# Two graph layers over 16 batches on one core: the first layer straight, squarings in six of eight pairs, and the second layer's prologue in the last two

## What is computed

```python
h = jnp.maximum(_layernorm(x), 0.0)
x = x + layer0(h, adj, alpha, w, d, fc_in_w, fc_in_b)
h = jnp.maximum(_layernorm(x), 0.0)
x = x + layer1(h, L=adj, adjacency=adj, ...)

# layer0: eight Euler steps, linear in h
ax = einsum('nm,bmd->bnd', adj, h)
f = alph * 0.5 * (ax - h) + h @ w_eff - h + x0
h = h + dt * f

# layer1
lam_max = eigvalsh(L)[-1] + 1e-08
L_norm = 2.0 * L / lam_max - eye(N)
h = relu(layernorm((L_norm @ x) @ Wc + bc)); x1 = h + x
scores = q @ k.T / sqrt(32)   # four heads, q, k, v = x1 @ Wq, Wk, Wv
attn = softmax(where(adjacency > 0, scores, -1e9))
x2 = layernorm(x1 + (attn @ v) @ Wo + bo)
return layernorm(x2 + gelu(x2 @ W1 + b1) @ W2 + b2)
```

## Time and profile before

| | us |
|---|---|
| median of 3 runs | 965.14 (964.48 to 966.01) |
| the profiled execution | 965.88 |
| its span | 964.1 |
| busy in it: PE, PEld, DVE, ACT, POOL | 885.7 (92%), 724.3 (75%), 653.7 (68%), 552.5 (57%), 325.2 (34%) |
| first layer with its setup | 0 to 443.6 |
| first mask of attention | 454.98 |
| POOL at the opening of the second block: L1682, L1665, L1667 | from 449.73: 1.28, 0.61, and 1.27 from 451.64 |
| landing of one load of x (256 KB), median | 2.8 |

### The profile page before, as it was taken

One profiled execution on the slowest core, in us unless ns is written; L12 is line 12 of the kernel. 1 busy time (PEld: TensorE's weight loads), 2 busy tenths in 40 slices (PEclk: granted clock), 3 DMA queues, 4 the chain that ended last, 5 costly groups with the idle time before them and its releaser, 6 DMA issues.

```text
span 964.1 us, 19623 instructions
## 1 busy us (share of the span) xinstructions
PE 885.7 (92%) x6854; PEld 724.3 (75%) x6854; DVE 653.7 (68%) x2077; ACT 552.5 (57%) x1210; POOL 325.2 (34%) x426
## 2 busy tenths in 40 slices
PE   5999999999999998984999999999999999888993
PEld 4878989898989888864777676767777777666782
DVE  5955343445444445544788888898888888887786
ACT  3223333333333333213888888888888887876574
POOL 3111111111120202121334545554555444313876
PEclk9999999999999998997999999999999999999998
DMA  3000000000000000005555544444445554500122
GB/s 96 0 12 12 12 12 13 11 12 12 11 11 11 22 0 12 1 1 131 131 133 133 133 122 113 110 112 104 110 125 131 132 133 133 130 4 1 47 64 66
DMA packets 47223, 61.61 MB, mean 64 GB/s; under 512 B 4377, under 2 KB 22050, under 8 KB 47138
## 3 DMA queue, kind: packets, MB, share of 16 engines
q1 hardware_dynamic: 46034, 60.38, 24.6%
q10 hardware_dynamic: 1104, 0.13, 0.1%
HBM read 39.53 MB, written 20.97 MB: 63 GB/s over the span
## 4 chain that ended last, share of the span: by engine, by line
PE 56%; DVE 13%; issue 10%; POOL 9%; ACT 7%; DMA 3%; SPq 0%; DVEq 0%; ACTq 0%; POOLq 0%
PE bank L828 10%; PE bank L798 9%; PE bank L790 9%; PE bank L782 6%; PE bank L1738 4%; DVE prob L1908 4%; PE bank L1758 3%; PE bank L694 2%; PE bank L1802 2%; POOL z_gain L333 2%; POOL z_norm L337 2%; DMA q_stack<-bounce_k 2%; ACT prob L1849 2%; PE bank L1725 2%; POOL x_bo L1682 2%
## 5 line engine op out<-in xcount | busy, mean ns | idle before, releaser
L1849 ACT ACTIVATE prob<-prob,low 128x512 f32<-128x512 f32 x256 | 183.9, 719 | 54.1 <-DVE low L1908 52.4
L1908 DVE CUSTOM_DVE_ANT_0 prob<-bank,mask 128x512 f32<-128x512 f32 x256 | 171.1, 682 | 27.0 <-PE bank L1725 25.7
L1738 PE MATMUL bank<-ident,prob 128*128 128x128 f32 x1024 | 161.8, 281 | 12.8 <-ACT probT L1838 12.8
L1738 PEld LDWEIGHTS bank<-ident,prob 128*128 128x128 f32 x1024 | 114.4, 141 | 58.5 <-issue 30.7
L1725 PE MATMUL bank<-k_stack,q_stack 128*128 128x512 f32 x256 | 123.7, 485 | 12.2 <-DMA q_stack<-bounce_k 9.2
L828 PE MATMUL bank<-B_hi,halves 128*128 128x384 f32 x384 | 107.7, 343 | 6.4 <-DVE halves L1176 6.4
L1838 ACT ACTIVATE probT<-bank 128x512 f32<-128x512 f32 x176 | 102.5, 583 | 2.8 <-PE bank L1738 1.1
L620 POOL TENSOR_SCALAR var_eps<-mv 128x4 f32<-128x4 f32 x16 | 3.6, 227 | 295.3 <-DVE mv L1127 295.3
L798 PE MATMUL bank<-halves,P3T_hi 128*128 128x256 f32 x512 | 95.8, 288 | 3.0 <-DVE halves L1194 1.8
L979 ACT ACTIVATE Sq<-bank,trace_inv 128x512 fp32r<-128x512 f32 x64 | 44.0, 687 | 91.4 <-PE bank L782 91.4
L1758 PE MATMUL bank<-probT,v 128*32 128x128 f32 x2048 | 82.3, 279 | 5.0 <-DVE probT L1895 1.7
(11 more groups left out here) (251 smaller groups left out, 1964.9 us busy)
## 6 DMA issues: line engine op xcount, KB each, us to landing
k_stack<-bounce_q SPq DMA_DIRECT2D x64, 256.0 KB, 5.0
q_stack<-bounce_k SPq DMA_DIRECT2D x64, 256.0 KB, 7.5
bounce_q<-k_parts SPq DMA_DIRECT2D x16, 512.0 KB, 2.8
bounce_k<-q_parts SPq DMA_DIRECT2D x16, 512.0 KB, 3.2
x_in<-in_x_dram SPq DMA_DIRECT2D x16, 256.0 KB, 2.8
out_dram<-probT SPq DMA_DIRECT2D x16, 256.0 KB, 2.3
y<-in_adj_dram SPq DMA_DIRECT2D x4, 256.0 KB, 4.3
W1s<-in_L_gnn_W_dram SPq DMA_DIRECT2D x1, 128.0 KB, 2.6
```

The lines of the kernel that those rows point to most:

```text
L1738: last = pe.transpose(psum[2 + u % 2][:, mt * P:(mt + 1) * P], prob[u % RING][:, mt * P:(mt + 1) * P], ident[:, :])
L1849: act.activation(prob[u % RING][:, :], prob[u % RING][:, :], ACT.Exp, bias=low[:, u % TURNED:u % TURNED + 1], scale=-1.0, accum_out=row_su ...
L1908: dve.tensor_tensor_reduce(prob[u % RING][:, :], psum[u % 2][:, :], mask[:, u // HEADS, :], 1.0, 3e38, ALU.add, ALU.min, low[:, u % TURNED ...
```

## The change

The first layer is written straight on all engines: the loops over pairs (and SP's over loads of x) become Python loops. The 16 squarings lie in pairs 0 to 5 (2, 3, 3, 3, 3, 2). What was early work of pair 7 is now in pair 6 (`LAM_PAIR`), and x1's transposes, keys and queries of batch 0 are in pair 7 (`KEY_PAIR`), one after another in bank 7, with waits for `k_lo_ready` and `q_lo_ready` ahead of the next user; values stay in pair 8. POOL takes batch 0's and 1's norm (`z_root`, `norm_z`) within pair 6, between the scales of batches 14 and 15, and h of batch 2 is made in pair 7. In `feature_products` the wait for T_lo[m] moves into the loop over m. The split of L moves from ahead of round 1 to its unit 1 (ACT) and unit 2 (DVE).

```diff
-def pairs(eng, body):
-    for p in range(3):
-        body(p)
-    with eng.Fori(3, LAST_SQUARED + 1) as p:
-        body(p)
-    for p in range(LAST_SQUARED + 1, PAIRS + 1):
-        body(p)
...
+SQUARES = (ROWS_FIRST, ROWS_3, ROWS_3, ROWS_3, ROWS_3, ROWS_2)
+TRACES = (("T0a", "C3a"), *[("T0a", "Y0_0", "C3a")] * 4, ("T0a", "C0a"))
+LAM_PAIR, KEY_PAIR = LAST_SQUARED + 1, LAST_SQUARED + 2
...
                 def pair(p):
-                    if isinstance(p, int) and p == PAIRS - 1:
+                    if p == LAM_PAIR:
                         for b in range(2):
                             h_scales(pool, one, b, b)
...
+                    x_and_bias(2 * p + 1, 1)
+                    if p == LAM_PAIR:
+                        z_root(pool, one, 0)
+                        norm_z(pool, one, 0)
+                        scales(2 * p + 2, 0)
+                        z_root(pool, one, 1)
+                        norm_z(pool, one, 1)
+                    if p < PAIRS - 1:
+                        scales(2 * p + 3, 1)
...
                 def feature_products(b, nt):
-                    if nt == 0:
-                        for m in range(GROUP):
-                            pe.wait_ge(T_lo_ready[m], b + 1)
                     at_least(pe, C_ready, NT * b + nt - 1)
                     for m in range(GROUP):
+                        if nt == 0:
+                            pe.wait_ge(T_lo_ready[m], b + 1)
...
-                    step = (p - (PAIRS - 1), place)
+                    step = (p - LAM_PAIR, place)
...
-                    if step == (0, "C3b"):
-                        x1_transpose(pe, one, psum[4], 0, 0)
+                    if step == (1, "T1a"):
+                        pe.wait_ge(one.z_ready, 2)
+                        x1_transpose(pe, one, SQ_BANK, 0, 0)
                     if step == (1, "Y1_0"):
-                        k_product(pe, one, psum[5], 0)
-                        q_product(pe, one, psum[6], 0)
-                    if step == (1, "Y1_1"):
-                        v_product(pe, one, psum[4], 0)
+                        k_product(pe, one, SQ_BANK, 0)
+                    if step == (1, "T2a"):
+                        pe.wait_ge(one.k_lo_ready, 1)
+                        q_product(pe, one, SQ_BANK, 0)
+                    if step == (2, "Y1_1"):
+                        pe.wait_ge(one.q_lo_ready, 1)
+                        v_product(pe, one, SQ_BANK, 0)
...
+AT_L_HI, AT_L_LO = (1, 1), (1, 2)
...
+                        if (r, u) == AT_L_HI:
+                            act.activation(L_parts[0][:, :, :], one.Lnorm[:, :, :], ACT.Copy).then_inc(L_hi_ready, 1)
...
-                act.activation(L_parts[0][:, :, :], one.Lnorm[:, :, :], ACT.Copy).then_inc(L_hi_ready, 1)
...
+                        if (r, u) == AT_L_LO:
+                            dve.wait_ge(L_hi_ready, 1)
+                            dve.tensor_tensor(out=L_parts[1][:, :, :], in0=one.Lnorm[:, :, :],
+                                              in1=L_parts[0][:, :, :].bitcast(F32), op=ALU.subtract).then_inc(L_lo_ready, 1)
...
-                dve.wait_ge(L_hi_ready, 1)
-                dve.tensor_tensor(out=L_parts[1][:, :, :], in0=one.Lnorm[:, :, :],
-                                  in1=L_parts[0][:, :, :].bitcast(F32), op=ALU.subtract).then_inc(L_lo_ready, 1)
```

## The result

The changed kernel took 951.88 us (median of 4 runs, 950.98 to 955.92), the kernel before 965.58 beside it (964.48 to 966.01, 4 runs). The ratio is 0.9849, with a 95% interval of 0.9821 to 0.9877. The profiled execution took 951.66 with a span of 949.9; the sum had come to 956.6 for it. So there are 4.9 us to explain.

The account below looks back on a forecast made before the run. The prediction took PE, busy 92% of the span, as the bound. Up to the block's end -8.9 and round 1 -0.4 gave -9.3 us: 956.6 for the profiled run, median 955.8, range 952.0 to 959.6.

Parts of the forecast that it names:

- The pairs: First layer, pairs 0 to 8: with fewer waits and moved work PE ends at 439.8, 3.8 us before 443.56.
- the wait itself: PE's wait for T's low part in the pairs: counted as its idle time only, 0.68 us.
- Straight code: Pairs 3 to 6, written out instead of looped: costs 0 to 0.8 us, 0.4 of it counted.
- The opening: Boundary behind the first layer: the block ends at 440.8 against 449.72, 8.9 us earlier.
- Round 1: Second layer's start, with the split of L moved inside: gains 0.4 to 1.5 us, taken as 0.4.
- a half-rate keys' product: Keys of batch 1: low part at +11.6 if the clock is half, +10.5 if full.
- The split's duration: DVE's split of L in round 1: 2.3 us with POOL's work done, against 3.39 before.
- Rival 2: The clock stays up in round 1, 954.3 us, and if also in pair 6, 952.2; chance 0.18.
- Rivals 3 to 5: 3, DVE/ACT late, 958 to 959.5, 0.18; 4, stacks late, 960.5 to 961, 0.04; 5, fetch late, about 990, 0.03.

Follow-up runs that it names:

- the second trace: Profile from measuring the changed kernel again, with nothing altered, beside the kernel before: 949.93 us, ratio 0.9821.
- the kernel with the old prologue: The kernel before with the wait per m and the split of L in round 1, but the prologue in its old place: 960.53 us, ratio 0.9933.
- the first trace: Profile from the changed kernel's first measurement, beside the kernel before: 951.88 us, ratio 0.9849.
- The second piece on DVE: The changed kernel with one more 128x2048 subtraction on DVE ahead of L_lo, its result unused: 955.01 us, ratio 0.988.
- the one in quarters: The changed kernel with the split of L done tile by tile in four quarters on ACT and DVE: 952.76 us, ratio 0.9844.
- the eigenvalue moved: The changed kernel with the products for v and the quotient behind Y1's halves: 946.83 us, ratio 0.9785; repeated, 947.43 us, ratio 0.9794.
- both changes: The changed kernel with the eigenvalue's products behind Y1's halves and the split of L in quarters: 947.1 us, ratio 0.9797.

## Why the prediction was right, and where it failed

**The pairs: right in kind, one term too small.** The mechanism (six products cover the wait) holds in pairs 0 to 5, and all but 0.4 of the wait is covered in 6 and 7. The term that was mis-sized is the wait itself: I took the idle time in front of the products, 0.68, and it is worth 0.93 with the slower restart behind it. So pairs 0 to 2 came 0.7 lower than in the sum (187.10 where it had 187.4, with a setup that was 0.4 longer), pairs 3 and 4 came to 47.9 instead of 48.16, pair 5 to 43.73 instead of 44.2, pair 6 to 55.2 instead of 56.0 and pair 7 to 38.6 instead of 39.0. Straight code cost none of its 0.4. The waits for L1164 left in pairs 6 and 7 are 0.4 where it had 0.6. Against this, pair 8 took 18.05 instead of 16.5, because the clock fell behind its wait of 2.2; in the second trace it didn't, and pair 8 took 16.6. The sum had not asked what the clock does there. Together the last product is 1.3 earlier than the sum had it.

**The opening: right.** The sum had the block open 1.0 behind PE's last product (440.8 and 439.8), and it did (439.5 and 438.47), where it had been 6.2. The reading that two things end late there, the stacks and behind them the split, is borne out by the kernel with the old prologue, where the first mask gains only the 1.4 that lie between the two.

**Round 1: the step that failed.** I gave it 0.4 to 1.5 and took 0.4; from the opening to the keys' DMA it went from 12.71 to 9.78 (2.9), and 3.0 is left at batch 15. The step that failed is the sentence that PE's scores of unit 4, with the keys behind them, wait for mask 3. They wait for mask 2 only: the scores ran at 443.10 and the keys' product at 445.48, before mask 3 at 446.48. I was off by one in how many masks the scores of a unit wait for, against the description of the kernel before, which has the scores of unit u + 1 wait for mask u - 1. The prediction put the scores, 0.5, and the keys' product, 0.9, in series behind mask 3; they lie in the shadow of the split, and behind mask 3 stands ACT's exponential, 0.7, instead. The keys' low part was to start at +10.5 with a full clock and started at +9.1: 0.4 of the 1.4 because mask 3 came at +7.0 and not at +7.4, 1.0 because of the path behind it. PE stood idle beside the split for 1.9 us and not for 3 to 4. The second part of the same mistake is the clock: the prediction added 1.1 (a half-rate keys' product), for it took it that PE falls to half and is waited for. (Its 0.4 is also not what its terms give: 12.0 less 11.6 is 0.4 already, and the clock's later return was to take 0.4 again, so nothing would be left.) In the first trace PE did not fall, in the second it did, and the keys came at the same 9.08 behind the first mask: an engine that isn't on the path may run at any rate. The second piece on DVE shows the path that is left, mask 3, exponential, high part on ACT, low part on DVE.

**The split's duration** was right: 2.29 with POOL idle, as L1101, not the 3.39 beside POOL's split of h. The keys of batch 2 went out 13.2 us earlier, where ten were forecast.

**The rivals.** Rival 2, 952.2 to 954.3, came nearest, but for the wrong reason: the clock stayed up in round 1 in one trace and fell in another with no difference, and in pair 6 it fell in every trace. Rivals 3 to 5 are refuted: no wait of pair 7 is above 0.4, the stacks were in time, straight code cost nothing. So the sign and most of the size are earned; how near the median comes to the range's edge is partly chance, since pair 8 alone differs by 1.5 us between two traces with the clock.

**Closing the 4.9 us:** 1.3 ahead of the last product, 2.6 in round 1, 0.9 behind the keys of batch 15, which is within what that stretch differs by from run to run.

## What to carry to other kernels

A wait can be worth more than the idle time in front of it, as 0.93 for 0.68 here: compare the same group of instructions behind the wait and without it. When a piece of work is put into an ordered loop, write down for each engine which instance of each signal it waits for, and walk all engines, for an off-by-one in one of them moves the critical path to another engine. And of two things that end late together, removing the one that ends last is worth only the distance to the other; moving the split of L gained nothing until the stacks were early too.

## What the runs showed of the hardware

**When the clock falls isn't fixed by the code.** The 32 one-column products of the eigenvalue follow a wait of 1.8 us. In two traces whose code is the same up to there they took:

```profile
L822 PE MATMUL bank<-v,S 128*128 128x1 f32 x32 | 4.1, 261 | 1.8 <-DVE v L1210 1.8
```

(the changed kernel) and

```profile
L822 PE MATMUL bank<-v,S 128*128 128x1 f32 x32 | 6.8, 348 | 1.8 <-DVE v L1210 1.8
```

(the one in quarters). In the first 3 us of these products the granted clock was 1.00 in the one and 0.53 in the other, and between these in the other traces; in the 3 us behind the products it was at 0.50 to 0.53 in all that keep the wait. With both waits taken away the products ran at 1.00 in two traces and the clock still fell behind them (0.71 and 0.72 in the two stretches of 3 us that follow, in the eigenvalue moved). In the third trace without the waits, that of both changes, it fell during the products (0.87 in their first 3 us, 0.50 behind them):

```profile
L822 PE MATMUL bank<-v,S 128*128 128x1 f32 x32 | 4.8, 284 | 0.0
```

So the fall isn't tied to recorded idle time alone: PE is busy in the records all the time there. What in these products lets it fall isn't separated. With the wait kept, pair 6 lay between 55.2 and 57.25, as much as an edit is worth: a single profile can't judge a change of 2 us in this kernel if the two differ in such a stretch.

**Restart.** Behind a wait of 0.7 us eighteen products took 0.26 more than without one, in looped pairs at a clock of 1.00, and the removal of the wait gave back 0.93 in all six pairs. The timeline of the kernel before has the first of them at 316.37 and the second 0.27 later, where the group without a wait has 0.18 between them; and that group's first starts at 320.51, 0.17 before the recorded end of the row of squaring ahead of it. These two differences make up the 0.26 (ends of matmuls are modelled in the records). What in the array or the weight loads causes them I haven't separated.
